# The vectors' products of a node update go from VectorE to GpSimd, and TensorE turns them later and in transpose mode

## The reference

```
a0 = agg[:, :64]
a1 = agg[:, 64:].reshape(n, 32, 3)
xs = node_features[:, :64]
xv = node_features[:, 64:].reshape(n, 32, 3)
u0 = jnp.einsum('nu,nv,uvw->nw', xs, a0, Wu_ss) * INV64 + jnp.einsum('nui,nvi,uvw->nw', xv, a1, Wu_vv) * (INV_SQRT3 * INV32)
u1 = jnp.einsum('nu,nvi,uvw->nwi', xs, a1, Wu_sv) * INV_SQRT2048 + jnp.einsum('nui,nv,uvw->nwi', xv, a0, Wu_vs) * INV_SQRT2048
u0 = u0 + xs @ Lu_s * INV8
u1 = u1 + jnp.einsum('nui,uw->nwi', xv, Lu_v) * INV_SQRT32
upd = jnp.concatenate([u0, u1.reshape(n, 96)], axis=-1)
return node_features + upd
```

## Time and profile before

| what | us |
|---|---|
| median of 3 runs | 20541.52 |
| lowest, highest | 20522.96, 20552.39 |
| the profiled execution | 20573.62 |
| its span in the trace | 20572.0 |
| TensorE, VectorE, ScalarE, GpSimd busy | 17578.1, 16081.1, 12429.6, 12351.1 |
| first and last `vv` of VectorE (line 1959, 100 in both stages) | 15665.4, 20545.7 |

### The profile page before, as it was taken

The page is one execution under the profiler, slowest core; times in us unless marked ns, Lnnn a source line. Parts: engine busy times, 40 slices in busy tenths (PEclk is TensorE's granted clock), DMA queues, the critical chain, the costliest instruction groups (busy, mean ns, idle before and its releaser), DMA issues. The chain is left out here.

```text
span 20572.0 us, 465117 instructions
## 1 busy us (share of the span) xinstructions
PE 17578.1 (85%) x121874; PEld 14135.8 (69%) x121874; DVE 16081.1 (78%) x44638; ACT 12429.6 (60%) x39738; POOL 12351.1 (60%) x13048
## 2 busy tenths in 40 slices
PE   2777666676699999999999999699998889999888
PEld 1333322222588888888888888699997669999766
DVE  3777799998588888888988888655556885555688
ACT  1222288887277777777777777267774226777422
POOL 2777777776367666666767676177772007777200
PEclk8888789888899999999999999999999999999999
DMA  2666577777744444444444444522222002222200
GB/s 83 170 171 171 164 136 142 140 141 127 240 121 123 122 121 122 122 121 122 124 123 123 122 121 122 140 64 67 67 67 30 6 6 63 67 67 67 30 6 6
DMA packets 1922898, 2132.27 MB, mean 104 GB/s; under 512 B 745584, under 2 KB 1597712, under 8 KB 1922544
## 3 DMA queue, kind: packets, MB, share of 16 engines
q0 software_dynamic: 567456, 1314.26, 24.1%
q1 hardware_dynamic: 1355344, 816.91, 16.1%
HBM read 1518.49 MB, written 611.44 MB: 104 GB/s over the span
## 5 line engine op out<-in xcount | busy, mean ns | idle before, releaser
L1639 POOL DMA_INDIRECT e_rows<-x,e_take x3456 | 3335.2, 965 | 1143.1 <-issue 1056.8
L1673 ACT ACTIVATE e_hot<-e_hot,e_here 128x128 f32<-128x128 f32 x10368 | 3123.5, 387 | 1389.2 <-DVE e_hot L1696 1381.3
L1659 PE MATMUL e_sums<-e_rows,e_hot 128*128 128x128 f32 x20736 | 2878.9, 275 | 0.0
L1659 PEld LDWEIGHTS e_sums<-e_rows,e_hot 128*128 128x128 f32 x20736 | 2678.9, 192 | 0.0
L632 PE MATMUL e_sums<-e_feat,e_same 128*128 128x480 f32 x3456 | 1761.3, 661 | 858.0 <-DVE e_feat L712 385.3
L615 POOL DMA_INDIRECT e_rows<-table,e_take x1728 | 1925.8, 1114 | 649.1 <-issue 620.9
L1214 ACT ACTIVATE e_m<-e_th,e_yt 128x64 f32<-128x64 f32 x6480 | 2301.3, 426 | 0.0
L1076 POOL DMA_INDIRECT e_srow<-src_table,e_at x1620 | 1615.2, 997 | 926.0 <-issue 917.8
L1087 POOL DMA_INDIRECT comb<-e_crow,e_at x1620 | 1664.6, 1028 | 823.7 <-issue 524.9
L771 POOL TENSOR_TENSOR n_stats<-n_stats,n_power 128x1 f32<-128x1 f32 x250 | 145.4, 582 | 3153.5 <-DVE n_stats L756 3066.4
L632 PEld LDWEIGHTS e_sums<-e_feat,e_same 128*128 128x128 f32 x3456 | 721.1, 219 | 1898.2 <-issue 1416.3
(11 more groups left out here) (331 smaller groups left out, 46900.9 us busy)
## 6 DMA issues: line engine op xcount, KB each, us to landing
e_pay<-pay_rows SPq DMA_DIRECT2D x432, 470.0 KB
order_keys<-key_row SPq DMA_DIRECT2D x810, 128.0 KB
e_keys<-key_row SPq DMA_DIRECT2D x810, 128.0 KB, 3.4
comb<-n_comb SPq DMA_DIRECT2D x600, 164.0 KB, 2.0
e_rows<-x,e_take POOLq DMA_INDIRECT x3456
order_feat<-in_attr_T SPq DMA_DIRECT2D x810, 64.0 KB
e_basis<-in_attr_T SPq DMA_DIRECT2D x1620, 32.0 KB
e_comps<-in_attr_T SPq DMA_DIRECT2D x1620, 32.0 KB
```

The lines of the kernel that those rows point to most:

```text
L1639: pool.indirect_dma_start(out=rows[t.j][:, q, 0:D], out_offset=None, in_=x, in_offset=bass.IndirectOffsetOnAxis(ap=take[t.j][:, q:q + 1], ...
L1659: ins = pe.matmul(bass.AP(o.tensor, o.offset, [o.ap[0], [DOT - CS * c, 2], [1, CS]]), one[:, q, 2 + c, :], bass.AP(r.tensor, r.offset, [r. ...
L1673: ins = act.activation(one[:, q, 2 + c, :], one[:, q, 0, :], ACT.Copy, scale=here[t.j][:, q, TOWARDS + c:TOWARDS + c + 1])
```

## The change

Four edits, all in `nodes_update`:

1. VectorE's instruction that makes `vv` is taken out of `pair_products`.
2. GpSimd makes `vv` with the same operands. In its step it stands behind the power of tile `p`, behind a wait for all four linked instructions of `finish(p)`, and behind the waits that VectorE had (row loaded, `agg_set`, and all halves of the tile before turned).
3. The matmuls that turn `vv` get `is_transpose=True`, still adding three components in PSUM.
4. TensorE turns half 8 behind `messages` of the next tile instead of ahead of contract 7; half 9 follows at once.

```
                             for k in range(3):
-                                ins = pe.matmul(to, vv[:, k * CV * CV + at:k * CV * CV + at + P], g.ident[:, :], start=k == 0, stop=k == 2)
+                                ins = pe.matmul(to, vv[:, k * CV * CV + at:k * CV * CV + at + P], g.ident[:, :], is_transpose=True,
+                                                start=k == 0, stop=k == 2)
...
                         for h in range(HALVES):
-                            if h < HALVES - 1:
+                            if h < 7 or h == 8:
                                 turn_half(b, h + 1)
...
                                 if s.exists():
                                     messages(s)
+                                turn_half(b, 8)
...
                     if p.exists():
                         inverse_root(pool, stats[p.j][:, 8:9], power[:, 0:1], squares, roots, p, 1, 1)
+                        pool.wait_ge(linked, p.count(4, 4))
+                    b = s.back(1)
+                    if b.exists():
+                        k = b.j
+                        pool.wait_ge(row_in[k], b.dma())
+                        pool.wait_ge(agg_set, b.count(1))
+                        if b.reuses(1):
+                            pool.wait_ge(half_ps, b.count(0, HALVES))
+                        pool.tensor_tensor(vv[:, :].rearrange("p (c u v) -> p c u v", c=3, u=CV),
+                                           bcast(row[k][:, CS:D].rearrange("p (c u) -> p c u", c=3).unsqueeze(3), (P, 3, CV, CV)),
+                                           bcast(agg[k][:, CS:D].rearrange("p (c v) -> p c v", c=3).unsqueeze(2), (P, 3, CV, CV)),
+                                           ALU.mult).then_inc(vv_set, 1)
...
-                    if b.reuses(1):
-                        dve.wait_ge(half_ps, b.count(0, HALVES))
-                    dve.tensor_tensor(vv[:, :].rearrange("p (c u v) -> p c u v", c=3, u=CV),
-                                      bcast(row[k][:, CS:D].rearrange("p (c u) -> p c u", c=3).unsqueeze(3), (P, 3, CV, CV)),
-                                      bcast(agg[k][:, CS:D].rearrange("p (c v) -> p c v", c=3).unsqueeze(2), (P, 3, CV, CV)),
-                                      ALU.mult).then_inc(vv_set, 1)
```

## The result

The changed kernel takes 20184.61 us (median of 4 runs, 20169.32 to 20188.2), the kernel before 20542.56 (median of 4, 20522.96 to 20552.39): a ratio of 0.9825, 95% interval 0.9811 to 0.984, or 358 us less. The forecast was 20193. The profiled execution took 20169.32, its span is 20167.6.

The account below looks back on a forecast made before the run. VectorE was taken to set the pace in a ring of waits with TensorE; 3.27 + 0.29 us less in each of 98 steps makes 349, so 20541.52 - 349 = 20193 us. The range was 20140 to 20400.

Parts of the forecast that it names:

- VectorE sets the step and loses 3.27 + 0.29: VectorE's step in a node stage: 3.27 us less without vv, 0.29 less in the normalisation, from 25.96 to 22.40.
- the second term: Normalisation, line 761: 0.29 us less a step, as GpSimd's copy no longer runs beside it.
- GpSimd's `vv`: Multiplication on GpSimd: 7.2 us taken, ends 3.6 and 7.8, free up to 9.0; the rival of a late GpSimd had 0.10.
- The sum: Whole kernel: 98 steps times 3.56 us, 349 less than the median of 20541.52, giving 20193.
- One pass in transpose mode: TensorE's vv halves: 24 passes instead of 48, 2.72 us for both; the rival of no saved passes had 0.07.
- TensorE keeps 1.2 us in hand: End of TensorE's step: ready at 22.5, while the next ss comes at 23.67, so VectorE is the bound.
- a wait of 0.7: TensorE at columns(b, 3): waits for VectorE's second product, done at 12.3, after contract 7 ends at 11.66.
- Holding: Rival: GpSimd's vv holds VectorE's first product, line 1988, and the step grows; 357 us slower, 20898, chance 0.06.
- rows 6 and 7: Profile rows: line 977, two SBUF inputs, took 1.01 beside a GpSimd copy; line 1338, one PSUM input, wasn't stretched at 0.35.
- The first tiles: First tile of each of two stages, vv starting together with ss: between -3.3 and +3.9 us each, taken as 0.
- 98 x 3.56 = 349: Total gain in us: 49 of 50 tiles in each of two stages gain 3.56 each.
- The clock: Rival: TensorE's clock falls to 0.79 as transposes replace vv's 48 passes; 190 us slower, 20730, chance 0.05.

Follow-up runs that it names:

- the copy behind the finish: Kernel before, plus only a GpSimd wait behind the power for the finish's four linked instructions, so its copy of own runs after the normalisation: 20518.83 us, 0.9983 of before.
- the products twice: Changed kernel, with GpSimd making the vv products twice, first into a spare buffer: 20588.71 us, 1.0016 of the kernel before.
- the run without the wait: Changed kernel without GpSimd's wait for the four linked instructions of the finish, so vv runs beside the normalisation: 20977.76 us, 1.0219 of the kernel before.
- the filled run: Kernel before with only vv's matmuls in transpose mode, plus 12 useless identity transposes ahead of each half of vv: 20528.06 us, 0.9999 of before.
- GpSimd's part: Kernel before with only vv moved to GpSimd with its wait, TensorE's order and two passes kept: 20844.8 us, 1.0142; with idle transposes 20641.76, 1.0035.
- the old order: Changed kernel with half 8 turned ahead of contract 7, columns and messages as before: 20596.93 us, 1.0023 of before; with idle transposes 20402.95, 0.9928.
- TensorE's part: Kernel before with only transpose mode and TensorE's new order, vv still made by VectorE: 20816.0 us, 1.0133 of before.

## Why the prediction was right

- *VectorE sets the step and loses 3.27 + 0.29.* Right: steps of 22.40 and 22.74 by turns, where 22.40 and 0.3 more at the loop's turn were to be had; the second term shown alone by the copy behind the finish.
- *GpSimd's `vv`.* 5.37, 1.75 ns a number, between the ends of 3.6 and 7.8, below the 7.2 that I took. The sum didn't hang on it, as the working says; with the products twice, at 10.7, the step does. The estimate of 6.7 us from the page "GPSIMD Engine Reference" of the Trainium skill, section "3.1 Elementwise — side-by-side cycle accounting", was nearer than 7.2 and also high.
- *One pass in transpose mode.* Right, 24 records a tile; 2.77 in place of 2.72.
- *TensorE keeps 1.2 us in hand.* Right, 1.20 measured; the columns took 1.62 instead of 1.06, where a wait of 0.7 was worked out.
- *Holding.* The first products of VectorE, with one input in PSUM, weren't held; the normalisation was, in the run without the wait. Both as rows 6 and 7 had it. The page "SBUF — State Buffer" of the Trainium skill, section "Who interferes with whom", says that a VectorE instruction in a two-port mode contends with GpSimd, and that one with at most one SBUF input outside these modes doesn't; the runs agree, 5.40 us for 0.36 against 1.75 to 1.76, though no row shows in which mode line 761 ran.
- *The first tiles.* I took 0, the middle between -3.3 and +3.9, and worked out nothing for it. That the two stages give 348.7 for 98 x 3.56 = 349 is luck to that extent. Beside GpSimd's first `vv` one `ss` of VectorE takes 6.38 us instead of 1.22. But before, VectorE waited 2.77 and 1.27 for TensorE in that tile of n4, and so the first step is still 1.1 (n3) and 0.2 (n4) shorter than before. The clock, at its lower level for a part of that tile in both kernels (0.92 and 0.90 over the first step before, 0.88 and 0.83 now), is in these numbers.
- *The clock* is the step that was right for too narrow a reason. I gave its fall 0.05 and looked for the cause in transposes in place of matmuls; the filled run shows that this was not it. What brings it down is time in which TensorE waits: in transpose mode alone, GpSimd's part and the old order idle work in place of the time without work put the clock back to 1.00. Three more versions have a clock below 0.95 and waits of 1.5 to 3.9 us (TensorE's part, the products twice, no wait for the finish); there nothing was filled. The length of the wait alone doesn't give the clock: before the change TensorE waits 1.64 for the row and 1.07 for `ss` in a step at 1.00, in TensorE's part alone 1.51 and 0.98 closer together at 0.84. In the change what TensorE saves, VectorE no longer makes it wait for: it waits 1.20 for `ss` and not at all for the row.

The parts don't add up: at full clock GpSimd's part alone loses 0.7 us a step, and the change gains 3.5. Transpose mode alone loses 1.4 with the clock at 0.93; what its saved work is worth at full clock without the other parts was not measured. Of the eight ways to combine the three parts, only the new order by itself has no run.

## What to carry to other kernels

Lay out one step of the bounding engines from the first instruction to the same one a step later, and ask of every moved instruction first when its result is wanted, then how long it takes: 5.37 us on an engine that had been busy for 54 of 1260 us cost nothing at one place in TensorE's order and the whole gain at another, half of that through the clock. Before taking work from TensorE, look at the wait that takes its place; where another engine set the pace, less work there was slower (1.0066 of before). VectorE's normalisation was held for the whole of GpSimd's `vv` where nothing ordered the two, so order two such instructions by a wait.

## What was not expected of the hardware

- With less work on TensorE the kernel got slower: a wait of 2.52 us in place of 1.07, and the granted clock of the stage fell from 1.00 to 0.93, at 0.63 right behind the wait. Waits of 3.08 and 3.15 went with 0.91 and 0.90.
- Where both VectorE and GpSimd start on two SBUF inputs, in the first tile, GpSimd is stretched too: `vv` 6.40 instead of 5.37, and its copy behind it 1.63 instead of 0.64, while two `ss` are held. One by one the three `ss` take 1.23, 6.38 and 1.65. The rows can be read as turns, each engine's next instruction standing until the other's is done: `vv` is 1.03 longer, and the first `ss` had 1.18 to go when it started:

```profile
15605.32 9.10 DVE L1968 TENSOR_TENSOR n_ss<-n_row,n_agg 128x1024 f32<-128x1024 f32 x3 [30.98 <-ACT n_a0T L1903]
```

```profile
15605.37 6.40 POOL L1946 TENSOR_TENSOR n_vv<-n_row,n_agg 128x3072 f32<-128x3072 f32 x1 [29.74 <-ACT n_a0T L1903]
15611.72 1.63 POOL L1934 COPY n_own<-acc 128x544 f32 x1
```
